# A transformer tower on one core: transfers of the first stage paced by tile, an edges' product over 128 rows, the shift on ScalarE, one more unread product

## The reference

```python
def reference(x, L0_tok_kernel, ...):
    # embedding over 8 vocabulary shards of 1575 rows; each shard clips the token to itself
    for start, W in zip(starts, kernel):                 # a scan in the source
        acc = acc + W[jnp.clip(x - start, 0, vs - 1)]
    h = acc + shards * bias + pos_emb                    # 4 x 512 x 1024
    # layernorm, attention with 32 heads over 8 kv heads of 128, causal
    h = h + attn(layernorm(h), w_qkv, w_dense)
    # layernorm, 16-headed MLP 64 -> 256 -> 64 on permuted features, exact gelu
    h = h + ffn(layernorm(h), up, down, perm)
```

## Time and profile before

| | |
|---|---|
| three timed executions | 2665.55, 2667.54, 2670.02 us |
| the profiled execution | 2666.3 us, its span 2664.5 us |
| PE busy | 2610.6 us, 98% of the span |
| weight loads of PE | 2108.4 us, 79% |
| DVE, ACT, POOL busy | 47%, 46%, 34% |
| mean granted clock of PE | 0.997 of full |
| DMA | 83 GB/s in the mean, 160 in the first fortieth of the span |

### The profile page before, as it was taken

How to read it: one execution, slowest core, us unless ns; L and a number is a source line. 1 busy time by engine, 2 the same in 40 slices (tenths; PEclk the granted TensorE clock), 3 DMA queues, 4 the chain that set the end, 5 groups by cost and what they waited for, 6 DMA issues and landing times.

```text
span 2664.5 us, 35848 instructions
## 1 busy us (share of the span) xinstructions
PE 2610.6 (98%) x12968; PEld 2108.4 (79%) x12968; DVE 1243.6 (47%) x3113; ACT 1232.9 (46%) x3056; POOL 906.4 (34%) x726
## 2 busy tenths in 40 slices
PE   8999999999999999999999999999999999999997
PEld 5888888888877777888887877788788777778883
DVE  4444444554544444455454443445545344444453
ACT  4544444454454554435445445544544444544432
POOL 4233334333334333433233333343332333333312
PEclk9999999999999999999999999999999999999999
DMA  4122224222322222522222232252222223222222
GB/s 160 57 71 72 72 72 129 79 64 62 98 79 91 74 75 82 141 72 68 68 88 83 83 92 76 76 141 64 72 83 76 76 87 91 86 69 68 72 72 83
DMA packets 112156, 221.24 MB, mean 83 GB/s; under 512 B 13358, under 2 KB 13358, under 8 KB 111982
## 3 DMA queue, kind: packets, MB, share of 16 engines
q1 hardware_dynamic: 104448, 193.52, 24.1%
q0 software_dynamic: 7424, 25.17, 3.3%
q10 hardware_dynamic: 110, 0.26, 0.0%
HBM read 202.13 MB, written 16.78 MB: 82 GB/s over the span
## 4 chain that ended last, share of the span: by engine, by line
PE 91%; DVE 4%; ACT 3%; issue 1%; DMA 1%; POOL 0%; ACTq 0%; DVEq 0%
PE fb L507 22%; PE fb L509 21%; PE fb L508 21%; PE tp L542 5%; PE sc L507 2%; PE sc L508 2%; PE sc L509 2%; PE sc L594 2%; PE fb L603 2%; PE pv L507 2%; PE pv L509 2%; PE pv L508 2%; ACT w_hi L746 1%; PE sc L533 1%; PE pv L556 1%; DVE pt_lo L901 1%
## 5 line engine op out<-in xcount | busy, mean ns | idle before, releaser
L1050 POOL TENSOR_TENSOR w_lo<-w_raw,w_hi 128x512 fp32r<-128x512 f32 x640 | 820.6, 1298 | 1596.8 <-ACT w_hi L746 1596.4
L507 PE MATMUL fb<-xn_hi,w_hi 128*128 128x512 f32 x1504 | 596.3, 396 | 2.0 <-DVE stats L949 1.7
L509 PE MATMUL fb<-xn_hi,w_lo 128*128 128x512 f32 x1504 | 587.5, 391 | 0.0
L508 PE MATMUL fb<-xn_lo,w_hi 128*128 128x512 f32 x1504 | 586.1, 390 | 0.0
L746 ACT ACTIVATE w_hi<-w_raw 128x512 fp32r<-128x512 f32 x640 | 383.3, 632 | 388.0 <-PE fb L509 377.8
L507 PE MATMUL fb<-at_hi,w_hi 128*128 128x512 f32 x992 | 394.4, 398 | 5.3 <-DVE hacc L944 3.6
L767 ACT ACTIVATE prob<-sc,neg_max 128x128 f32<-128x128 f32 (+3 forms) x512 | 263.4, 527 | 284.9 <-DVE neg_max L889 284.3
L509 PE MATMUL fb<-at_hi,w_lo 128*128 128x512 f32 x992 | 387.6, 391 | 0.0
L508 PE MATMUL fb<-at_lo,w_hi 128*128 128x512 f32 x992 | 386.9, 390 | 0.0
L507 PEld LDWEIGHTS fb<-xn_hi,w_hi 128*128 128x128 f32 x1504 | 282.4, 188 | 78.7 <-issue 18.8
L944 DVE TENSOR_TENSOR hacc<-hacc,fb 128x512 f32<-128x512 f32 x256 | 175.7, 686 | 339.2 <-PE fb L509 338.6
(11 more groups left out here) (195 smaller groups left out, 3537.0 us busy)
## 6 DMA issues: line engine op xcount, KB each, us to landing
w_raw<-in_w_qkv SPq DMA_DIRECT2D x384, 256.0 KB, 2.7
w_raw<-in_w_dense SPq DMA_DIRECT2D x256, 256.0 KB, 2.6
h_rows<-hacc SPq DMA_DIRECT2D x32, 256.0 KB, 2.3
h_tok<-in_pos SPq DMA_DIRECT2D x12, 512.0 KB, 5.9
mlp_w<-in_w_mlp SPq DMA_DIRECT2D x24, 256.0 KB, 3.0
first_pos<-in_pos SPq DMA_DIRECT2D x4, 512.0 KB, 7.3
end_w<-in_w_mlp SPq DMA_DIRECT2D x8, 256.0 KB, 4.6
token_row<-in_x_row SPq DMA_DIRECT2D x8, 64.0 KB, 7.0
```

The costliest lines, as they stand in the source:

```text
L507: pe.matmul(dst, a_hi, b_hi, start=first, stop=False)
L508: pe.matmul(dst, a_hi, b_lo, start=False, stop=False)
L509: return pe.matmul(dst, a_lo, b_hi, start=False, stop=last)
L1050: pool.tensor_tensor(w_lo[:, m % RW, :], w_raw[:, m % RAW, :], w_hi[:, m % RW, :], ALU.subtract)\
```

## The change

SP waits for all six transfers of edge rows before it issues the positions of tile 1, and weight 1 goes behind the positions of tile 2. POOL's gathers of tiles 2 and 3 wait for the arrival of the gather two before. `edges` and `coef` get 128 partitions; two memsets on DVE zero the rows 64 to 127, and the product L691 runs over all 128, in all four batches. DVE no longer computes the shift: in `La` it writes the negated mean, and ACT, in front of each tile's normalisation, multiplies it by `rstd` in a copy with a scale and waits for its own result, again in all batches. There is one more `w` at the start, before the first `B`. The rounding of weight 5 is moved from step Lb2 to X4.

```diff
-START = ("A G0 G1 G2 G3 w0 w1 J0 J1 B0 B1 La0 B2 Lb0 B3 La1 J2 X0 X1 w2 Lb1 C0 B4 B5 La2 J3 X2 X3 Lb2 C1 w3 B6 B7 La3 "
+START = ("A G0 G1 G2 G3 w0 w1 w2 J0 J1 B0 B1 La0 B2 Lb0 B3 La1 J2 X0 X1 w3 Lb1 C0 B4 B5 La2 J3 X2 X3 Lb2 C1 w4 B6 B7 La3 "
          "X4 X5 Lb3 a0 C2 a1 X6 X7 C3 a2 a3 Q0 K Q1 V VT")
 FIRST_SPLITS = [Step(k, 0, 0, i) for k, i in (
-    ("B", 1), ("Lb", 0), ("X", 1), ("Lb", 1), ("X", 3), ("Lb", 2), ("X", 5), ("Lb", 3), ("X", 7), ("C", 3), ("Q", 0))]
+    ("B", 1), ("Lb", 0), ("X", 1), ("Lb", 1), ("X", 3), ("X", 4), ("X", 5), ("Lb", 3), ("X", 7), ("C", 3), ("Q", 0))]
...
-        edges = sb("edges", [64, E], F32R)
+        edges = sb("edges", [P, E], F32R)
         with ExitStack() as own:
-            token_row = sb("token_row", [64, S], I32, own)
-        coef = sb("coef", [64, S], F32R)
+            token_row = sb("token_row", [P, S], I32, own)
+        coef = sb("coef", [P, S], F32R)
+        neg_mean = sb("neg_mean", [P, TT], F32)
...
             first_positions(0)
+            sp.wait_ge(edge_in, 96)
             first_positions(1)
             load(0)
-            load(1)
             sp.wait_ge(pos_in[0], 16)
             first_positions(2)
+            load(1)
...
-                    pe.matmul(first_bank((0, 1, 5, 6)[s.i]), ones[:, :], mask[:, :], start=True, stop=True)
+                    pe.matmul(first_bank((0, 1, 2, 5, 6)[s.i]), ones[:, :], mask[:, :], start=True, stop=True)
...
+                act.activation(shift[:, c:c + 1], neg_mean[:, c:c + 1], copy, scale=rstd[:, c:c + 1])\
+                   .then_inc(shift_done, 1)
+                act.wait_ge(shift_done, TT * b + c + 1)
                 if b > 0:
                     act.activation(normal(b, c), h_tok[:, c, :], ACT.Identity,
                                    scale=rstd[:, c:c + 1], bias=shift[:, c:c + 1]).then_inc(row_ready, 1)
...
                 elif s.kind == "Lb":
-                    act.wait_ge(shift_done, tally.la[Step("La", *s[1:])] + 1)
+                    act.wait_ge(mean_ready, tally.la[Step("La", *s[1:])] + 1)
+                    act.wait_ge(rstd_done, tally.la[Step("La", *s[1:])] + 1)
                     normalise_tokens(s.b, s.i % TT)
...
+            dve.memset(coef[64:P, :].bitcast(F32), 0.0).then_inc(edge_step, 1)
+            dve.memset(edges[64:P, :].bitcast(F32), 0.0).then_inc(edge_step, 1)
...
-                elif s.kind == "Lb":
-                    cs = slice(s.i, s.i + 1) if s.i < TT else slice(0, TT)
-                    dve.wait_ge(rstd_done, tally.la[Step("La", *s[1:])] + 1)
-                    dve.scalar_tensor_tensor(out=shift[:, cs], in0=moments[:, cs, 0], scalar=-1.0, in1=rstd[:, cs],
-                                             op0=ALU.mult, op1=ALU.mult).then_inc(shift_done, 1)
+                    dve.tensor_scalar(neg_mean[:, cs], moments[:, cs, 0], -1.0, None, ALU.mult).then_inc(mean_ready, 1)
...
                     if s.b == 0:
+                        if s.i > 1:
+                            pool.wait_ge(gathered[s.i - 2], 16)
                         pool.indirect_dma_start(out=h_tok[:, s.i, :], out_offset=None, in_=table, in_offset=token)\
                             .then_inc(gathered[s.i], 16)
```

More of the change, by code:

```diff
@@ L353, in tower_kernel @@
         shift_done = sem("shift_done")
+        mean_ready = sem("mean_ready")
         rstd_done = sem("rstd_done")
@@ L655, in _ @@
                 elif s.kind == "w":
-                    if s.i == 3:
+                    if s.i == 4:
                         pe.wait_ge(first_free, 1)
-                    pe.matmul(first_bank((0, 1, 5, 6)[s.i]), ones[:, :], mask[:, :], start=True, stop=True)
+                    pe.matmul(first_bank((0, 1, 2, 5, 6)[s.i]), ones[:, :], mask[:, :], start=True, stop=True)
                 elif s.kind == "d":
@@ L684, in _ @@
                     if s.b == 0 and s.i == 0:
-                        pe.wait_ge(edge_step, 3)
+                        pe.wait_ge(edge_step, 5)
                     if s.b > 0 and s.i == 0:
@@ L861, in _ @@
             dve.tensor_scalar(rows[:, :], xi[:, :], 0, VOCAB - 1, ALU.max, ALU.min).then_inc(rows_ready, 1)
+            dve.memset(coef[64:P, :].bitcast(F32), 0.0).then_inc(edge_step, 1)
+            dve.memset(edges[64:P, :].bitcast(F32), 0.0).then_inc(edge_step, 1)
             def coefficients():
-                return dve.tensor_scalar(coef[:, :], token_row[:, :], edge_consts[:, 0:1], edge_consts[:, 1:2],
+                return dve.tensor_scalar(coef[0:64, :], token_row[0:64, :], edge_consts[:, 0:1], edge_consts[:, 1:2],
                                          ALU.mult, ALU.is_ge)
@@ L870, in _ @@
             dve.wait_ge(edge_in, 96)
-            dve.tensor_copy(edges[:, :], edge_rows).then_inc(edge_step, 1)
-            dve.wait_ge(edge_step, 2)
+            dve.tensor_copy(edges[0:64, :], edge_rows).then_inc(edge_step, 1)
+            dve.wait_ge(edge_step, 4)
             dve.tensor_tensor(edges[32:64, :], edge_rows[32:64, :], edges[32:64, :], ALU.subtract).then_inc(edge_step, 1)
```

## The result

| | before | after |
|---|---|---|
| timed executions of this comparison | 2667.95 us median (2665.55 to 2670.02, 4) | 2650.68 us median (2649.57 to 2651.64, 4) |
| profiled execution, its span | 2666.3, 2664.5 | 2650.18, 2648.4 |

The ratio is 0.9939, with the 95% interval 0.9927 to 0.9951: 17.3 us by the medians, 16.1 by the two profiled executions. The forecast was 2653.0, a gain of 13.3: 2.3 above the measured median, and 2.8 above the profiled execution that it was summed against. The measured time lies inside the range.

The account below looks back on a forecast made before the run. PE, busy 98% of the span, was taken to bound the kernel, with a chain of waits in its first 34 us. Rows 8.2, shift 1.65 and head 3.5 sum to 13.3; 2666.3 - 13.3 = 2653.0 us, range 2648.5 to 2660.

Parts of the forecast that it names:

- What bounds the kernel: Whole kernel: PE, busy 98% of the span, sets the time; in the first 34 us a chain of waits does.
- Rows, 8.2: Edges' product in the stream over 128 rows: 0.34 us saved on each of 24, 8.2 together; ends 0 and 9.6.
- Shift in the stream, 1.65: Three token stages: first tile gains 0.85 us each, 2.55; fourth loses 0.3 each, 0.9; net gain 1.65.
- The head, 3.5: Start up to the first projection: it begins at 30.2 us, not 33.75, a gain of 3.5; ends 0 and 6.
- The gather: Head: first embedding gather lands 0 to 1.3 us earlier, 1.0 taken; first addition at 10.75, not 11.76.
- The second positions: Head: issued 3.1 us later, they land at 12.2 to 15.5, 13.2 taken; second addition then runs 13.2 to 14.5.
- The low clock: Head: PE's clock still falls to 1.2 GHz until 16.8; if it stays up, first two sums about 2 us earlier.
- Rival C: Head and stream: clock holds and first gather comes early; head gains 6, stream 10.5, total 2650 us; chance 0.15.
- rival A: Edges' product: rows don't matter, it still costs 0.57 us; 4.4 gained in all, 2662 us; chance 0.08.
- DVE's shift held by POOL: Head, tile 2: DVE's one-column shift took 1.27 us beside POOL's w_lo; moving it to ACT leaves 0.8 gain.
- D: Rival, every tile: ACT's scaled copy needs function table loads, 1283 ns each, two per tile; slower, 2679 us; chance 0.03.
- B: Rival, head: gives nothing, second positions land at 15.5, clock low, projections start at 33.7; 2656.5 us; chance 0.14.

Follow-up runs that it names:

- shifts_at_once: The changed kernel with all four shifts of a token stage in the stream taken on ACT at its first tile; 2650.59 us, ratio 0.9939.
- rows_alone: The kernel before with only the edges' product run over 128 rows instead of 64; 2657.44 us, ratio 0.9963.
- shift_alone: The kernel before with only the shift moved to ACT, computed from DVE's negated mean; 2664.57 us, ratio 0.9989.
- after_again: The changed kernel unaltered, timed again on the same chip as the kernels with one part left out; 2649.83 us, ratio 0.9939.
- all_but_pacing: The changed kernel without the transfers' pacing: SP's and POOL's waits removed, weights in the old order; 2651.26 us, ratio 0.9942.
- product_alone: The kernel before with only one more unread product in front; 2668.20 us, ratio 1.0004.

## Why the prediction was right, and where it was off

1. *What bounds the kernel.* Right: PE's stream, the first token tile's chain in the head, three short stalls. No part moved another engine to the bound.
2. *Rows, 8.2.* Measured 8.7 (2.90, 2.90 and 2.89 in after; 8.65 alone). Right in mechanism, and 0.02 per product low.
3. *Shift in the stream, 1.65.* Measured 1.56: +0.84 and -0.28 in the first stage, and net 0.54 and 0.46 in the two others. Both signs were forecast and both were there. shifts_at_once shows that the loss was the one instruction in front of row_buf.
4. *The head, 3.5.* Measured 6.5 and 6.1, the step that was mis-sized. Up to the first tile's transposes 3.84 (and 3.12) against 1.7, behind it 2.64 (3.00) against 1.8. Four terms:
   - The gather was given at most 1.3, since no packet of its queue moves before 7 us in the trace of before. That took one profile for a fixed start: in the thirteen others the queue has packets in the microsecond from 6, with pacing and without. The profile's gain was 2.5; by the means of the profiles without and with SP's order it is 1.2. The bound was wrong, and that the mean is near the 1.0 taken is luck. The second positions, taken to land at 13.2, landed at 12.06, which is what the first tile's statistics waited for.
   - The low clock was taken as unchanged to 16.8. It was low for 3.4 us instead of 6.8, so the two first sums took 3.3 (10.53 to 13.85) where 4.1 was summed. Only with both the unread product and SP's order was it that short. Rival C, that clock and gather both come out well, was closer for the head: 6.
   - The edges' products of the head have no term in the head's sum, though rival A prices all eight at 0.8. rows_alone gains 1.50 between the first transposes and the first projection, where four of the eight stand. shift_alone gains 1.93 there, near the 1.8 forecast for the shift; the whole gains less than the two together.
   - DVE's shift held by POOL: right in kind. The earlier trace rows show 1.27 beside w_lo; now neg_mean takes 0.13 at 22.68 while w_lo runs on POOL from 22.02 to 23.29, and the addition at 22.74 takes 1.63 instead of 1.23. The old shift and the addition read two tiles in SBUF, neg_mean reads one. The Trainium skill ("SBUF — State Buffer", Who interferes with whom) says that a DVE instruction with two SBUF inputs contends with a GpSimd instruction that reads SBUF. The three rows agree with it.
5. *The end, not forecast.* Small and of both signs: after loses 1.06 after 2610, after_again, the same kernel, 0.11. It goes by how long the clock was low there, 6.8 and 3.4 us. What decides between the two the runs don't show.
6. *The rivals.* A (rows don't matter) and D (a table load per tile) are out: before and after have 64 table loads each, and no shift of after is longer than 0.31. B (2656.5) fell with the positions that landed at 12.06.

Sum by measured terms: 6.48 + 8.69 + 1.56 = 16.7, 0.5 of small gains spread over the stream, less 1.06 in the end: 16.2, the profiled difference. Against the forecast of 13.3 that is +3.0 in the head, +0.5 in the rows, +0.5 of small gains, -0.1 in the shift and -1.1 in the end.

Open: how much of the unread product's effect in the head is its own, and what the move of the rounding of weight 5 gives. The head's profiles vary by more than a us with the landing of the first gather and of the second positions, and one profile each can't settle a clock's place.

## What to carry to other kernels

Where one small product with fewer rows stands between products over all 128, fill its operands with zeros: 0.36 us each came back, and nothing else changed. Where the start waits for one transfer, look at what the other queues move beside it, and hold back what isn't needed next: the order on the issuing engine was enough, waits on the queue itself gave nothing. See then which transfer is next to be waited for; here it was the one held back. One profile per version is not enough in such a place: the first addition differed by 1.9 us between kernels whose transfers were issued alike. An early sum at a low clock is a late one: the pacing alone showed 0.3 us of lead. A clock held at its full level gave nothing visible in the head, where a transfer set the pace, and in the end, where PE's products were on the path, filling the idle time brought 1.9 us.

## What the runs showed of the hardware that was not expected

- The gathers' queue moves nearly nothing while another queue fills the engines: from 6 to 7 us 0 to 0.03 MB beside q1 at 91 to 100% (before, shift_alone, all_but_pacing), 0.15 and 0.16 MB beside 54 and 64% (product_alone, rows_alone).
- Four one-column instructions in a row on ACT took 0.85 us together, 0.19 from start to start; one with its own wait costs 0.31.
- The end of the kernel, the same code in all profiles but those with its idle time filled, lost 0, 1.05 or 2.1 us of lead with 3.4, 6.8 or 10.2 us of low granted clock; filling the idle time before it with unread products brought 1.9 us.
